# Adding two halves of a softmax's exponents on GpSimd, so that TensorE sums one half, a step later

## The chip, the cores and the metric

One core of one Trainium2 chip runs the whole program. The metric is the device time of one execution in microseconds (us). The core has five engines with queues of their own: TensorE (PE, its weight loads as PEld), VectorE (DVE), ScalarE (ACT), GpSimd (POOL) and SyncE (SP, which here only issues DMAs). They meet at semaphores alone.

## The reference

The kernel computes a gated block over 64 batches of 256 positions by 512 columns, in float32: cross attention with 16 heads of 32 columns on a normalised `x`, then a gated feed-forward part.

```
att = einsum('bthf,byhf->bhty', relu(q), relu(k))      # q = layernorm(x), k = v = ctx
att = softmax(att / sqrt(32), axis=-1)
out = einsum('bhty,byhf->bhtf', att, relu(v))
x = x + tanh(g_xattn) * relu(out @ ffn_w.T + ffn_b)
# second part, on layernorm(x): r = sigmoid(xr @ W_r.T), k = xk @ W_k.T
x = x + tanh(g_ffn) * (r * (square(relu(k)) @ W_v.T))
```

## The kernel before

Each engine runs one function `iteration(i, par)` for i from -3 to 66; the middle ones are a loop over pairs. Inside an iteration the order on each engine is written out by hand, and nothing else sets it: an engine runs its list in order and waits where a semaphore is not yet high enough. Batch i is in attention, batch i-1 in its projection, batch i-2 in the feed-forward part, batch i+1 begins its scores.

TensorE's iteration has 16 steps, each opened by `shifted_scores(i, n)` (L933) for head n = 0 to 15. The other pieces lie between: `scores(i+1, n)` or `scores(i, n)` (L921, whose row maxima VectorE takes), quarters of the dense products `dense(q, part)` (L966), transposes, and for each group c of four heads `values(i, c)` (L947: exponents times values) and `denominators(i, c)` (L959: exponents times ones). The last two write the two halves of one PSUM bank, `pv_bank`. A head's exponents are 128 keys by 2 halves `v` by 256 queries, so both sum over the two key halves by accumulating in PSUM; a group has 8 matmuls for its values and 8 for its denominators, each of which the trace shows as two records.

Who waits for whom around the third group (c = 2) of an iteration:

- ScalarE writes the exponents (L509) into `probs`, half 0 for even groups, half 1 for odd ones.
- VectorE's `norm_o(i, 2)` waits for the third denominators, takes the reciprocal (L737, 1 instruction) and multiplies (L739). Only then may TensorE's `values(i, 3)`, in the next iteration's step 0, overwrite `pv_bank`.
- VectorE's `head_max(i+1, n)` (L718) reduces the scores of L921; `finish(i-2, 0)` is L788 and L791; `k_low` is L707; `q_low` L701; `mix_k` L771, `mix_r` L780; `add_x` begins with L746.
- GpSimd's list ends with `xk_low(i-1, 0)`, `xk_low(i-1, 1)` (both L379) and `o_low(i, 0)` (L361). The second `xk_low` waits for ScalarE's second `xk_high` (L540).
- ScalarE issues `load_v(i+1, 0)`, a DMA, after the third denominators; its `exponent(i, 15)` and `o_high(i, 0)` (L516) stand behind that.
- SP's `write_o(i, 2)` follows `norm_o(i, 2)`.

Of the kernel before, what the change touches and what calls it, by code (L numbers as in the profile page):

```python
# [7 lines left out]
ALU = mybir.AluOpType  # L8
# [8 lines left out]
def flamingo_block(nc, x, ctx_in, ctx_t, g_xattn, g_ffn, w_t, bias, mu, out):  # L17
# [18 lines left out]
    NB, T, D = x.shape  # L36
    HD = D // HEADS
    NU = T // P
    KC = D // P
    GR = P // HD  # L40
    CH = HEADS // GR
    SCALE = float(HD) ** -0.5
    assert NU == 2 and KC == 4 and GR == 4 and CH == 4 and HD == 32
# [4 lines left out]
    with es:  # L48
# [104 lines left out]
        m_copied = sem("m_copied")  # L153
        st_ready = sem("st_ready")
        exp_ready = sem("exp_ready")
        pv_ready = sem("pv_ready")
        rden_ready = sem("rden_ready")
        o_ready = sem("o_ready")
# [174 lines left out]
        def _(pool):  # L333
# [39 lines left out]
            def xk_low(b, half):  # L373
                if on(b):
# [4 lines left out]
                    nc.gpsimd.tensor_tensor(xk_lo[:, part, :], xm[:, part, :], xk_hi[:, part, :].bitcast(F32),  # L379
                                            ALU.subtract).then_inc(xk_lo_ready, 1)  # L380

            def xr_low(b):
                if on(b):
                    pool.wait_ge(xr_ready, b + 1)
                    pool.wait_ge(xr_hi_ready, b + 1)
                    after(pool, r_ready, NU * b)
                    nc.gpsimd.tensor_tensor(xr_lo[:, :, :], xd[:, :, :], xr_hi[:, :, :].bitcast(F32),  # L387
                                            ALU.subtract).then_inc(xr_lo_ready, 1)
# [17 lines left out]
            def iteration(i, par):  # L406
                ka_square(i - 2, 0)
                rstd_1(i + 2)
                ka_square(i - 2, 1)
                o_low(i - 1, 1)  # L410
                xr_low(i - 2)
                rstd_2(i - 1, 0)
                rstd_2(i - 1, 1)
                x_diff(i - 1, 0)
                ka_low(i - 2, 0)
                ka_low(i - 2, 1)
                x_diff(i - 1, 1)
                xk_low(i - 1, 0)
                xk_low(i - 1, 1)
                o_low(i, 0)  # L420

            pipeline(pool, iteration)
# [235 lines left out]
        def _(dve):  # L658
# [135 lines left out]
            def iteration(i, par):  # L794
# [54 lines left out]
                finish(i - 2, 0, par)  # L849

                head_max(i + 1, 5)
                norm_o(i, 2)

                head_max(i + 1, 6)

            dve.wait_ge(setup_act, 2)
            nc.vector.tensor_scalar(tgh[:, :], tg[:, 1:2], 0.5, None, ALU.mult).then_inc(setup_dve, 1)
# [5 lines left out]
        def _(pe):  # L863
# [73 lines left out]
            def values(b, c):  # L937

                if on(b):
                    pe.wait_ge(exp_ready, HEADS * b + GR * c + GR)  # L940
                    pe.wait_ge(v_ready, 2 * b + 1 + c // 3)

                    after(pe, o_ready, CH * b + c)
                    for v in range(NU):
                        for g in range(GR):
                            h = GR * c + g
                            nc.tensor.matmul(pv_bank[HD * g:HD * g + HD, 0:T], v_pos[:, v, HD * h:HD * h + HD],  # L947
                                             probs[:, c % 2, g, v, :], start=(v == 0), stop=(v == NU - 1))

            def denominators(b, c):  # L950


                if on(b):

                    after(pe, o_ready, CH * b + c)
                    sums = [[probs[:, c % 2, g, v, :] for g in range(GR)] for v in range(NU)]
                    for n, per_head in enumerate(sums):
                        for g, moving in enumerate(per_head):
                            mm = nc.tensor.matmul(pv_bank[HD * g:HD * g + HD, T:2 * T], ones_r[:, 0:HD].bitcast(F32),  # L959
                                                  moving, start=(n == 0), stop=(n == len(sums) - 1))  # L960
                    mm.then_inc(pv_ready, 1)
# [65 lines left out]
            def iteration(i, par):  # L1027
# [121 lines left out]
                shifted_scores(i, 14)  # L1149
                dense(7, 0)  # L1150
                scores(i + 1, 5)
                denominators(i, 2)
                dense(7, 1)

                shifted_scores(i, 15)
                dense(7, 2)
                scores(i + 1, 6)
                dense(7, 3)

# [37 lines left out]
```

## Time and profile before

| | |
|---|---|
| median of 3 runs | 2789.77 us (2787.65 to 2789.96) |
| the profiled execution | 2788.89 us, of which 2787.0 us from its first to its last instruction |
| TensorE busy | 2681.2 us, 96% |
| VectorE busy | 2298.6 us, 82% |
| ScalarE busy | 1464.3 us, 53% |
| GpSimd busy | 1079.4 us, 39% |
| DMA | 576.71 MB, mean 207 GB/s |
| mean granted TensorE clock | 0.994 |

The table gives shares over the whole span. Matmuls are pipelined and overlap in the trace, so the end of one lies behind the start of the next; what a piece costs TensorE is read from start to start. The program does the same thing about every 41.4 us, so one iteration, read instruction by instruction, stands for most of the run.

### The profile page before, as it was taken

The numbers are of one execution on the slowest core, as the hardware profiler recorded it, in microseconds if no ns is written. First come the engines' busy times: TensorE is split into PE (matmuls) and PEld (weight loads), VectorE is DVE, ScalarE is ACT, GpSimd is POOL, SyncE is SP. The second block draws the span as 40 slices with busy tenths as digits, with TensorE's granted clock in tenths as the row PEclk, the third lists the DMA queues.
The fourth block names the chain that finished last, engine by engine and source line by source line (L and its number), as shares of the span: only waits on it lengthen the run. The fifth ranks groups of instructions, "written<-read, shape, count | busy, mean of one in ns | idle before, by whom it ended". The sixth has DMA issues, their size and how long they took to land.

```text
span 2787.0 us, 65658 instructions
## 1 busy us (share of the span) xinstructions
PE 2681.2 (96%) x21250; PEld 2056.1 (74%) x21250; DVE 2298.6 (82%) x3981; ACT 1464.3 (53%) x2507; POOL 1079.4 (39%) x902
## 2 busy tenths in 40 slices
PE   1799999999999999999999999999999999999998
PEld 1477777777777777777777777777777777777776
DVE  3778888888888888888888888888888888888864
ACT  2445555555555555555555555555555555555542
POOL 0134334443444433434434434434443444343433
PEclk9899999999999999999999999999999999999999
DMA  7676677677777677677677677777777667767641
GB/s 220 182 214 198 199 225 211 204 236 211 200 231 219 199 231 217 201 228 215 206 221 218 204 222 223 204 217 226 208 208 234 210 202 231 216 201 226 195 121 44
DMA packets 507774, 576.71 MB, mean 207 GB/s; under 512 B 175824, under 2 KB 407248, under 8 KB 507728
## 3 DMA queue, kind: packets, MB, share of 16 engines
q1 hardware_dynamic: 355152, 341.18, 41.7%
q10 hardware_dynamic: 152576, 234.93, 27.9%
q8 instruction: 27, 0.44, 0.1%
q14 instruction: 19, 0.16, 0.0%
HBM read 373.56 MB, written 201.33 MB: 206 GB/s over the span
## 4 chain that ended last, share of the span: by engine, by line
PE 89%; DMA 4%; DVE 2%; SPq 2%; issue 1%; ACT 1%; POOL 1%; ACTq 0%; DVEq 0%; POOLq 0%
PE bank L966 50%; PE bank L933 9%; PE bank L947 9%; PE bank L959 9%; PE bank L921 8%; PE bank L908 3%; PE bank L891 2%; DMA o_mv<-o_dram 2%; PE bank L899 1%; DMA o_dram<-o_val 1%; DMA q_st<-m_t 1%; DVE o_val L737 1%; SPq L291 1%; DVE m_nat L718 0%; ACT xr_hi L546 0%
## 5 line engine op out<-in xcount | busy, mean ns | idle before, releaser
L509 ACT ACTIVATE probs<-bank 128x512 f32<-128x512 f32 x1024 | 610.4, 596 | 898.7 <-PE bank L933 875.1
L718 DVE TENSOR_REDUCE m_nat<-bank 128x2 fp32r<-128x512 f32 x1024 | 687.9, 683 | 119.8 <-PE bank L921 119.2
L737 DVE RECIPROCAL o_val<-bank 128x256 f32<-128x256 f32 x256 | 449.3, 1755 | 108.5 <-PE bank L959 101.7
L921 PE MATMUL bank<-k_st,q_st 96*128 96x256 f32 x2048 | 431.8, 293 | 19.0 <-DVE m_nat L718 12.1
L933 PE MATMUL bank<-q_st,k_st 97*128 97x256 f32 x2048 | 426.4, 290 | 23.6 <-DMA q_st<-m_t 22.7
L933 PEld LDWEIGHTS bank<-q_st,k_st 97*128 97x128 f32 x2048 | 356.4, 191 | 104.2 <-issue 28.4
L921 PEld LDWEIGHTS bank<-k_st,q_st 96*128 96x128 f32 x2048 | 358.3, 192 | 73.0 <-DVE m_nat L718 15.9
L379 POOL TENSOR_TENSOR xk_lo<-xm,xk_hi 128x512 fp32r<-128x512 f32 x128 | 211.4, 1652 | 269.0 <-DVE xm L771 234.7
L394 POOL TENSOR_TENSOR xm<-xm 128x512 f32<-128x512 f32 x128 | 133.8, 1046 | 452.2 <-ACT xm L553 452.1
L966 PE MATMUL bank<-xk_hi,w_hi 128*128 128x256 f32 x1024 | 294.9, 288 | 0.0
L361 POOL TENSOR_TENSOR o_lo<-o_mv,o_hi 128x512 fp32r<-128x512 f32 x128 | 167.6, 1310 | 326.5 <-ACT o_hi L516 320.2
L966 PE MATMUL bank<-xk_hi,w_lo 128*128 128x256 f32 x1024 | 286.6, 280 | 0.0
L966 PE MATMUL bank<-xk_lo,w_hi 128*128 128x256 f32 x1024 | 286.6, 280 | 0.0
L947 PE MATMUL bank<-probs,v_pos 128*32 128x256 f32 x4096 | 275.8, 387 | 1.0 <-DVE o_val L739 1.0
L959 PE MATMUL bank<-probs,ones_r 128*32 128x256 f32 x4096 | 276.3, 387 | 0.0
L353 POOL TENSOR_TENSOR rstd<-ve,mhalf 128x1 f32<-128x1 f32 x128 | 69.2, 540 | 450.5 <-DVE ve L755 450.5
L966 PE MATMUL bank<-w_hi,o_hi 128*128 128x512 f32 x512 | 209.4, 409 | 17.4 <-POOL o_lo L361 17.4
L966 PE MATMUL bank<-w_hi,xr_hi 128*128 128x512 f32 x512 | 209.0, 408 | 4.2 <-POOL xr_lo L387 4.2
L966 PEld LDWEIGHTS bank<-xk_hi,w_hi 128*128 128x128 f32 x1024 | 192.6, 188 | 26.0 <-issue 25.9
L966 PE MATMUL bank<-w_hi,ka_hi 128*128 128x512 f32 x512 | 209.7, 410 | 0.0
L966 PE MATMUL bank<-w_hi,ka_lo 128*128 128x512 f32 x512 | 203.7, 398 | 0.0
L966 PE MATMUL bank<-w_hi,xr_lo 128*128 128x512 f32 x512 | 203.6, 398 | 0.0
(87 smaller groups left out, 5445.1 us busy)
## 6 DMA issues: line engine op xcount, KB each, us to landing
q_st<-q_dram ACTq DMA_DIRECT2D x256, 256.0 KB, 4.9
k_st<-k_dram SPq DMA_DIRECT2D x256, 256.0 KB, 4.6
x_ln<-x_dram SPq DMA_DIRECT2D x256, 128.0 KB
k_raw<-ctx_t_dram SPq DMA_DIRECT2D x256, 128.0 KB, 5.0
q_dram<-q_high ACTq DMA_DIRECT2D x64, 512.0 KB, 3.1
q_dram<-q_raw ACTq DMA_DIRECT2D x64, 512.0 KB, 4.1
k_dram<-k_high SPq DMA_DIRECT2D x64, 512.0 KB, 4.4
k_dram<-k_raw SPq DMA_DIRECT2D x64, 512.0 KB, 5.4
```

Of the source, the lines that this page charges most:

```text
L361: nc.gpsimd.tensor_tensor(by_tile(o_lo, u), o_mv[:, :, :].rearrange("p g (k a) -> p k g a", k=KC), by_tile(o_hi, u).bitcast(F32), ALU.subt ...
L379: nc.gpsimd.tensor_tensor(xk_lo[:, part, :], xm[:, part, :], xk_hi[:, part, :].bitcast(F32), ALU.subtract).then_inc(xk_lo_ready, 1)
L394: nc.gpsimd.tensor_tensor(part, part, part, ALU.mult).then_inc(ka_ready, 1)
L509: nc.scalar.activation(probs[:, n // GR % 2, n % GR, :, :].rearrange("p v t -> p (v t)"), st_bank[n % 2][:, :], ACT.Exp, scale=SCALE).then ...
L718: nc.vector.tensor_reduce(m_nat[:, c % 2, n % GR, :], s_bank[n % 2][:, :].rearrange("p (u y) -> p u y", u=NU), AX_X, ALU.max, negate=True) ...
L737: nc.vector.reciprocal(o_val[:, c % 2, :], pv_bank[:, T:2 * T]).then_inc(rden_ready, 1)
L908: mm = nc.tensor.transpose(tp_bank[:, P * c:P * c + P], xn[:, u, P * c:P * c + P], ident_r[:, :].bitcast(F32))
L921: mm = nc.tensor.matmul(s_bank[n % 2][:, T * u:T * u + T], q_st[0:QK, c, g, P * u:P * u + P], k_st[0:QK, c, g, :], start=True, stop=True)
L933: mm = nc.tensor.matmul(st_bank[n % 2][:, T * v:T * v + T], k_st[0:ST, c, g, P * v:P * v + P], q_st[0:ST, c, g, :], start=True, stop=True)
L947: nc.tensor.matmul(pv_bank[HD * g:HD * g + HD, 0:T], v_pos[:, v, HD * h:HD * h + HD], probs[:, c % 2, g, v, :], start=(v == 0), stop=(v == ...
L959: mm = nc.tensor.matmul(pv_bank[HD * g:HD * g + HD, T:2 * T], ones_r[:, 0:HD].bitcast(F32), moving, start=(n == 0), stop=(n == len(sums) - 1))
L966: mm = nc.tensor.matmul(dst, lhs[a], rhs[c], start=first and n == 0, stop=last and n == 2, skip_group_check=True)
```

## The change

Three edits. GpSimd gets a function `fold(i)`, between the second `xk_low` and `o_low(i, 0)`: after TensorE's third values have read `probs`, it adds the exponents of the second key half to those of the first, in place (128 partitions by 4 heads by 256 queries, 1024 elements in each partition). TensorE's third denominators then sum over the first half alone: 4 matmuls in place of 8; they wait for the fold, and stand in step 15, behind `dense(7, 2)`, in place of step 14. On VectorE `head_max(i+1, 6)` now stands ahead of `norm_o(i, 2)`. Two semaphores are new, `v_used` and `p_folded`.

```diff
@@ -38,6 +38,7 @@
     NU = T // P
     KC = D // P
     GR = P // HD
+    FOLDED = 2
     CH = HEADS // GR
     SCALE = float(HD) ** -0.5
     assert NU == 2 and KC == 4 and GR == 4 and CH == 4 and HD == 32
@@ -153,6 +154,8 @@
         m_copied = sem("m_copied")
         st_ready = sem("st_ready")
         exp_ready = sem("exp_ready")
+        v_used = sem("v_used")
+        p_folded = sem("p_folded")
         pv_ready = sem("pv_ready")
         rden_ready = sem("rden_ready")
         o_ready = sem("o_ready")
@@ -379,6 +382,13 @@
                     nc.gpsimd.tensor_tensor(xk_lo[:, part, :], xm[:, part, :], xk_hi[:, part, :].bitcast(F32),
                                             ALU.subtract).then_inc(xk_lo_ready, 1)
 
+            def fold(b):
+
+                if on(b):
+                    pool.wait_ge(v_used, b + 1)
+                    half = [probs[:, FOLDED % 2, :, v, :] for v in range(NU)]
+                    nc.gpsimd.tensor_tensor(half[0], half[0], half[1], ALU.add).then_inc(p_folded, 1)
+
             def xr_low(b):
                 if on(b):
                     pool.wait_ge(xr_ready, b + 1)
@@ -417,6 +427,7 @@
                 x_diff(i - 1, 1)
                 xk_low(i - 1, 0)
                 xk_low(i - 1, 1)
+                fold(i)
                 o_low(i, 0)
 
             pipeline(pool, iteration)
@@ -849,9 +860,9 @@
                 finish(i - 2, 0, par)
 
                 head_max(i + 1, 5)
+
+                head_max(i + 1, 6)
                 norm_o(i, 2)
-
-                head_max(i + 1, 6)
 
             dve.wait_ge(setup_act, 2)
             nc.vector.tensor_scalar(tgh[:, :], tg[:, 1:2], 0.5, None, ALU.mult).then_inc(setup_dve, 1)
@@ -944,8 +955,10 @@
                     for v in range(NU):
                         for g in range(GR):
                             h = GR * c + g
-                            nc.tensor.matmul(pv_bank[HD * g:HD * g + HD, 0:T], v_pos[:, v, HD * h:HD * h + HD],
-                                             probs[:, c % 2, g, v, :], start=(v == 0), stop=(v == NU - 1))
+                            mm = nc.tensor.matmul(pv_bank[HD * g:HD * g + HD, 0:T], v_pos[:, v, HD * h:HD * h + HD],
+                                                  probs[:, c % 2, g, v, :], start=(v == 0), stop=(v == NU - 1))
+                    if c == FOLDED:
+                        mm.then_inc(v_used, 1)
 
             def denominators(b, c):
 
@@ -953,7 +966,9 @@
                 if on(b):
 
                     after(pe, o_ready, CH * b + c)
-                    sums = [[probs[:, c % 2, g, v, :] for g in range(GR)] for v in range(NU)]
+                    if c == FOLDED:
+                        pe.wait_ge(p_folded, b + 1)
+                    sums = [[probs[:, c % 2, g, v, :] for g in range(GR)] for v in range(1 if c == FOLDED else NU)]
                     for n, per_head in enumerate(sums):
                         for g, moving in enumerate(per_head):
                             mm = nc.tensor.matmul(pv_bank[HD * g:HD * g + HD, T:2 * T], ones_r[:, 0:HD].bitcast(F32),
@@ -1149,11 +1164,11 @@
                 shifted_scores(i, 14)
                 dense(7, 0)
                 scores(i + 1, 5)
-                denominators(i, 2)
                 dense(7, 1)
 
                 shifted_scores(i, 15)
                 dense(7, 2)
+                denominators(i, 2)
                 scores(i + 1, 6)
                 dense(7, 3)
 
```

TensorE's list in the first iteration of the loop, before, from the third `values` (L947) to the next iteration's `values` (a `shifted_scores` is L933, a `scores` L921, a dense quarter three rows of L966):

```order
649 L933 MATMUL bank<-q_st,k_st 128x256 x2
650 L966 MATMUL bank<-w_hi,ka_hi 128x512
651 L966 MATMUL bank<-w_hi,ka_lo 128x512
652 L966 MATMUL bank<-w_lo,ka_hi 128x512
653 L921 MATMUL bank<-k_st,q_st 128x256 x2
654 L959 MATMUL bank<-probs,ones_r 32x256 x8
655 L966 MATMUL bank<-w_hi,ka_hi 128x512
656 L966 MATMUL bank<-w_hi,ka_lo 128x512
657 L966 MATMUL bank<-w_lo,ka_hi 128x512
658 L933 MATMUL bank<-q_st,k_st 128x256 x2
```

and the same stretch after the change, a little further on, where L974 is the denominators, L981 a dense quarter, L944 and L932 the two kinds of scores:

```order
653 L932 MATMUL bank<-k_st,q_st 128x256 x2
654 L981 MATMUL bank<-w_hi,ka_hi 128x512
655 L981 MATMUL bank<-w_hi,ka_lo 128x512
656 L981 MATMUL bank<-w_lo,ka_hi 128x512
657 L944 MATMUL bank<-q_st,k_st 128x256 x2
658 L981 MATMUL bank<-w_hi,ka_hi 128x512
659 L981 MATMUL bank<-w_hi,ka_lo 128x512
660 L981 MATMUL bank<-w_lo,ka_hi 128x512
661 L974 MATMUL bank<-probs,ones_r 32x256 x4
662 L201 REGISTER_ALU
663 L932 MATMUL bank<-k_st,q_st 128x256 x2
```

The third denominators have moved behind two dense quarters and a `shifted_scores`, and are four matmuls. They stand right ahead of `scores(i+1, 6)`.

VectorE's list at the same place, before (L718 is `head_max`, L788 and L791 are `finish(i-2, 0)`, L737 and L739 `norm_o(i, 2)`):

```order
281 L788 SCALAR_TENSOR_TENSOR th<-th,bank 128x512
282 L791 SCALAR_TENSOR_TENSOR x<-th,tgh,x 128x512
283 L713 REGISTER_ALU
284 L718 TENSOR_REDUCE m_nat<-bank 128x2
285 L737 RECIPROCAL o_val<-bank 128x256
286 L739 TENSOR_TENSOR o_val<-bank,o_val 128x256
287 L713 REGISTER_ALU
288 L718 TENSOR_REDUCE m_nat<-bank 128x2
```

and after (L729, L799, L802, L748 and L750 are the same five):

```order
280 L799 SCALAR_TENSOR_TENSOR th<-th,bank 128x512
281 L802 SCALAR_TENSOR_TENSOR x<-th,tgh,x 128x512
282 L724 REGISTER_ALU
283 L729 TENSOR_REDUCE m_nat<-bank 128x2
284 L724 REGISTER_ALU
285 L729 TENSOR_REDUCE m_nat<-bank 128x2
286 L748 RECIPROCAL o_val<-bank 128x256
287 L750 TENSOR_TENSOR o_val<-bank,o_val 128x256
```

The reciprocal and its product now stand behind the maximum of head 6, whose scores TensorE makes after the denominators.

## Rows read from the trace of the kernel before

**Rows 1.** The page: busy us, share and instructions of each engine.
```profile
PE 2681.2 (96%) x21250; PEld 2056.1 (74%) x21250; DVE 2298.6 (82%) x3981; ACT 1464.3 (53%) x2507; POOL 1079.4 (39%) x902
```

**Rows 2.** Busy time by stretch: PE, PEld, DVE, ACT, POOL (instructions), clock, DMA.
```profile
1500.00:1550.00 50.00, 50.00 (x404) 37.80 (x403) 42.34 (x79) 28.42 (x49) 20.05 (x19) 1.00 0.68 203
```

**Rows 3.** Timeline of PE around the third denominators: start, duration, operation.
```profile
1507.25 1.07 PE L959 MATMUL bank<-probs,ones_r 128*32 128x256 f32 x16
...
1517.53 0.40 PE L921 MATMUL bank<-k_st,q_st 96*128 96x256 f32 x2
1517.87 1.07 PE L959 MATMUL bank<-probs,ones_r 128*32 128x256 f32 x16
1518.87 0.50 PE L966 MATMUL bank<-w_hi,ka_hi 128*128 128x512 f32 x1
1519.20 0.40 PE L966 MATMUL bank<-w_hi,ka_lo 128*128 128x512 f32 x1
...
1520.59 0.40 PE L921 MATMUL bank<-k_st,q_st 96*128 96x256 f32 x2
...
1522.82 1.07 PE L947 MATMUL bank<-probs,v_pos 128*32 128x256 f32 x16
```

**Rows 4.** Of the same denominators, the last eight records, then the last four.
```profile
1518.32 0.61 PE L959 MATMUL bank<-probs,ones_r 128*32 128x256 f32 x8
...
1518.54 0.40 PE L959 MATMUL bank<-probs,ones_r 128*32 128x256 f32 x4
```

**Rows 5.** Timeline of POOL at that place.
```profile
1516.75 1.69 POOL L379 TENSOR_TENSOR xk_lo<-xm,xk_hi 128x512 fp32r<-128x512 f32 x1 [0.96 <-issue]
1521.35 1.28 POOL L361 TENSOR_TENSOR o_lo<-o_mv,o_hi 128x512 fp32r<-128x512 f32 x1 [2.91 <-ACT o_hi L516]
```

**Rows 6.** Timeline of DVE at that place, and at the denominators before.
```profile
1508.38 1.76 DVE L737 RECIPROCAL o_val<-bank 128x256 f32<-128x256 f32 x1 [0.37 <-PE bank L959]
...
1516.08 1.20 DVE L707 SCALAR_TENSOR_TENSOR k_raw<-k_raw,k_high 128x1024 fp32r<-128x1024 f32 x1
1518.51 0.75 DVE L791 SCALAR_TENSOR_TENSOR x<-th,tgh,x 128x512 f32<-128x512 f32 x1
1519.18 0.68 DVE L718 TENSOR_REDUCE m_nat<-bank 128x2 fp32r<-128x512 f32 x1
1519.78 1.75 DVE L737 RECIPROCAL o_val<-bank 128x256 f32<-128x256 f32 x1
1521.57 0.42 DVE L739 TENSOR_TENSOR o_val<-bank,o_val 128x256 f32<-128x256 f32 x1
```

**Rows 7.** Groups of POOL by form: count, busy us, mean ns, idle before and releasers.
```profile
L379 POOL TENSOR_TENSOR xk_lo<-xm,xk_hi 128x512 fp32r<-128x512 f32 x128 | 211.4, 1652 | 269.0 <-DVE xm L771 234.7 <-issue 33.7 <-ACT xk_hi L540 0.6
L387 POOL TENSOR_TENSOR xr_lo<-xd,xr_hi 128x1024 fp32r<-128x1024 f32 x64 | 152.4, 2382 | 10.7 <-issue 10.1 <-ACT xr_hi L546 0.2
L394 POOL TENSOR_TENSOR xm<-xm 128x512 f32<-128x512 f32 x128 | 133.8, 1046 | 452.2 <-ACT xm L553 452.1
L370 POOL TENSOR_TENSOR xd<-xt 128x512 f32<-128x512 f32 x128 | 133.2, 1041 | 5.3 <-ACT xt L531 2.2
```

**Rows 8.** Timeline near the end: DVE's L791 beside POOL's two `xk_low`.
```profile
2755.23 2.55 POOL L379 TENSOR_TENSOR xk_lo<-xm,xk_hi 128x512 fp32r<-128x512 f32 x2 [1.71 <-DVE xm L771]
...
2756.51 1.82 DVE L791 SCALAR_TENSOR_TENSOR x<-th,tgh,x 128x512 f32<-128x512 f32 x1
```

**Rows 9.** PE and POOL where PE waits for POOL.
```profile
2575.63 1.26 POOL L361 TENSOR_TENSOR o_lo<-o_mv,o_hi 128x512 fp32r<-128x512 f32 x1 [5.93 <-ACT o_hi L516]
2577.04 0.47 PE L966 MATMUL bank<-w_hi,o_hi 128*128 128x512 f32 x1 [3.06 <-POOL o_lo L361]
```

**Rows 10.** PE at the first group: the scores right behind its denominators.
```profile
1537.46 0.51 PE L933 MATMUL bank<-q_st,k_st 97*128 97x256 f32 x2
```

**Rows 11.** Clock around waits of PE: a stretch with a wait of 2.03, one with 3.06.
```profile
196.00:212.00 16.00, 13.97 (x92) 10.40 (x94) 9.63 (x17) 7.78 (x14) 5.21 (x4) 0.89 0.68 175
2572.00:2584.00 12.00, 8.94 (x63) 6.91 (x63) 6.86 (x13) 7.06 (x13) 4.21 (x3) 1.00 0.62 150
```

## The prediction

> **What bounds the kernel now.** I read the page's busy shares first: TensorE 96%, VectorE 82%, GpSimd 39% [rows 1]. A share over the whole span leaves open whether TensorE ever waits, so next came the busy time by stretch: in the middle of the run TensorE is busy 50.00 of 50.00 us at a granted clock of 1.00 [rows 2]. Its list has no hole there, so what is taken out of it, or made to wait in it, counts in full. Then I read one iteration in order of time, TensorE first and after it the two engines on which the change makes it wait [rows 3, 5, 6]. The reader is to see how little lies between the pieces: GpSimd's second `xk_low` ends at 1516.75 + 1.69 = 1518.44 [rows 5], TensorE begins the third denominators at 1517.87 and the fourth group's `values`, already in the next iteration, at 1522.82 [rows 3], and VectorE ends `norm_o(i, 2)`, for which those values wait, at 1521.57 + 0.42 = 1521.99 [rows 6]. That is 0.83 us to spare.
>
> **What is saved.** The sixteen records of the third denominators take 1.00 us from their start to the next matmul's [rows 3], in packs of four; the last two packs start at 1518.32 and 1518.54 [rows 4], 0.22 apart. Two packs less save 0.44 us an iteration, and 0.56 is left.
>
> **When TensorE would come to the denominators.** Six equal units of dense work and scores stand between 1519.20 and 1520.59 [rows 3], so one takes 0.23. The denominators add 1.00, and beside it 0.11 ahead (1517.53 to 1517.87 is 0.34 for one unit) and 0.10 behind (1518.87 to 1519.20 is 0.33 for one) [rows 3]: 1.21. Taken out of step 14 they let TensorE reach the place ahead of `scores(i+1, 6)` at 1520.59 - 1.21 = 1519.38, and with the 0.11 the moved denominators could start at 1519.48.
>
> **When the fold is done.** It stands behind the second `xk_low` and can't start before 1518.44. That is late for a reason that stays: `xk_low` needs VectorE's `mix_k`, that stands behind `norm_o(i, 1)`, and this waits for TensorE's second denominators in the same iteration (0.37 us idle ahead of L737 at 1508.38, which is 0.06 after 1507.25 + 1.07) [rows 3, 6]. A TensorE that waits in step 15 thus gives GpSimd no lead. The fold's duration is in no row: 1024 elements, float32 written. With `fp32r` written, 512 take 1.28 [rows 5] and 1024 take 2.38 [rows 7], so 0.18 is fixed and 1.10 goes with every 512. With float32 written, 512 take 1.04 (L370, L394) [rows 7]; less 0.18 that is 0.86, and twice 0.86 with 0.18 is 1.90. I take 1.90, as the fold writes float32 like these two. It can't be under the 1.04 of half the elements, and 2.38 is the nearest whole operation of that size; these are its ends. So it ends at 1520.34, and a TensorE that waits for GpSimd starts 0.15 later (2575.63 + 1.26 = 2576.89, then 2577.04) [rows 9]: at 1520.49, a wait of 1.01 us.
>
> For this size the Trainium skill has a price of its own: GPSIMD Engine Reference, section "Performance versus the Vector engine", gives an add of 2048 float32 elements 4497 ns some 2.6 cycles an element, and calls that the floor for two inputs; half of 4497 is an estimate of 2.25 us. The 1.04 of 512 elements with float32 written [rows 7] lies under a quarter of it (1.12). By the page each iteration would lose 0.35 more, and the run would end at 2915.
>
> **What VectorE does meanwhile.** L791 of `finish` starts at 1518.51 [rows 6], with the fold. It reads two SBUF tensors, and such an instruction and GpSimd's do not run side by side: beside `xk_low`, which ends at 2755.23 + 2.55 = 2757.78, L791 took from 2756.51 to 2758.33, 1.82 in place of the 0.75 that it takes alone [rows 6], and ended 0.55 after it [rows 8]; the other way round, `xk_low` began at 1516.75 inside `k_low` (L707, 1516.08 to 1517.28) and ended 1.16 after that one's end, for an operation that alone takes 1.28 [rows 5, 6]. Whoever starts second waits. The fold is 0.07 us ahead, so L791 ends at 1520.34 + 0.55 = 1520.89 and `head_max(i+1, 5)` about 0.6 later, at 1521.5. I cost this at nothing, since the next maximum has to wait for TensorE anyhow, as follows.
>
> **The second wait.** Behind the denominators (1520.49) `scores(i+1, 6)` start 0.56 later, at 1521.05, and last 0.51, as scores behind denominators do [rows 10]: 1521.56. `head_max(i+1, 6)`, now ahead of `norm_o(i, 2)`, starts 0.06 after, at 1521.62, and gives way 0.60 later (1519.18 to 1519.78) [rows 6]; `norm_o` takes 1519.78 to 1521.99, 2.21 [rows 6], and ends at 1524.43. `values(i, 3)` start at 1524.49. Unhindered TensorE would be there 0.56 + 0.10 + 2.23 (1520.59 to 1522.82) after the denominators [rows 3], at 1523.38; it waits 1.11.
>
> **The sum.** `values(i, 3)` move from 1522.82 to 1524.49, +1.67 us, which is 1.01 + 1.11 - 0.44. From there the iteration is as before: the next denominators and `norm_o(i, 3)` follow at the same distance. What else moves has room: ScalarE's `load_v` waits for the later denominators, and `exponent(i, 15)`, `o_high` and GpSimd's `o_low` stand behind it. Before, `o_low` started 2.41 after the denominators' end (1518.94 to 1521.35) [rows 3, 5]; at that distance it starts at 1523.5 and ends at 1524.8, ahead of `norm_o(i, 3)`, which needs it and can't come before `values(i, 3)` and the denominators behind it, 1.07 and 1.07 long [rows 3]. On SP `write_o(i, 2)` is later by 2.4, and behind it stands a `move_m` that depends on a still later maximum. Of 64 iterations I count 62, as the first and the last have not all their neighbours: 62 x 1.67 = 104 us. The profiled execution took 2788.89, so 2892; the median of the runs is 0.88 above it, so 2893. With the fold at 1.04 an iteration loses 0.81 (2840), with 2.38 it loses 2.15 (2923).
>
> **Rivals.**
> - VectorE gets the memory first. The fold's lead is 0.07 us, and its first read may come later than its start. Then it stands until L791 ends at 1519.26 and, like `xk_low`, needs 0.12 less than its 1.90 from there: 1521.04, 0.70 later than above; 2.37 an iteration, 147 in all, 2937. For it speaks the narrow lead, against it that the fold has by then nothing else to wait for. 14%.
> - The fold is hidden, and only VectorE's new order costs. It would have to end by 1519.33, 0.89 us after it can start, less than 512 elements take [rows 7]. TensorE then starts the denominators at 1519.48, `values(i, 3)` come at 1523.48, +0.66: 41 us, 2831. 7%.
> - Faster: TensorE's waits let the other engines get ahead, neither wait is left, and the saved 0.44 shows: 62 x 0.44 = 27, 2762. For it speaks that GpSimd is 39% and VectorE 82% busy [rows 1]; it decides once `xk_low` ends a good 1.0 earlier in TensorE's terms and `norm_o` 1.1 earlier. Against it stands the wait of VectorE for the second denominators [rows 6], which ties them to TensorE every time. 5%.
> - The clock falls as well. After a wait of TensorE of 2.03 us the granted clock was 0.89 over 16.00 us, some 1.8 us lost, and after one of 3.06 it stayed 1.00 [rows 11]. The two waits here are about half as long, 3 us apart. If every second iteration paid it, 55 us more: 2948. 6%.
>
> **Chances and range.** The forecast has 66%, the four rivals 14, 7, 5 and 6, and 2% is for waits and saving that balance. A difference under 0.2%, some 5.6 us, can't be told from no change here. Slower by more than that: forecast, first, second and fourth rival, 93%; within it 2%; faster 5%. The likeliest case alone runs from 2871 to 2923 (a fold of 1.55 to 2.38); with the first rival's 2937 and some room at the lower end for a shorter fold the range is 2850 to 2945, and the hidden fold, the clock and the faster case are left outside.
>
> **What would show it.** In the profile after: TensorE idle ahead of the third denominators, released by GpSimd's fold, some 1.0 us each time; idle again ahead of the values, released by L739's successor, some 1.1; a fold of about 1.9 us; L791's successor at a mean of about 1.6 in place of 0.75, as one of its two per iteration takes some 2.4; the granted clock still near 1. A fold over 2.5 us with an unchanged L791 is the first rival. No wait ahead of the denominators makes the prediction wrong, and no wait ahead of the values makes it wrong by two thirds.

## The result, and the profile after

The changed kernel takes 2902.05 us (median of 4 runs, 2900.70 to 2902.94) against 2789.39 us of the kernel before (4 runs, 2787.65 to 2789.96): a ratio of 1.0405, 95% interval 1.0389 to 1.0420. The forecast was 2893 within 2850 to 2945, so the direction and nearly the size are as foretold. The profiled execution took 2901.61 us, its span 2899.5.

The page's busy line and the chain that ended last, of the changed kernel, and below the same chain before (the busy line before is [rows 1]):

```profile
PE 2656.5 (92%) x20738; PEld 2032.9 (70%) x20738; DVE 2449.3 (84%) x3981; ACT 1462.0 (50%) x2507; POOL 1231.6 (42%) x966
...
PE 62%; DVE 14%; issue 11%; POOL 5%; DMA 2%; ACT 2%; ACTq 2%; SPq 1%; DVEq 0%; POOLq 0%
```

```profile
PE 89%; DMA 4%; DVE 2%; SPq 2%; issue 1%; ACT 1%; POOL 1%; ACTq 0%; DVEq 0%; POOLq 0%
```

TensorE does 24.7 us less, in 512 instructions less, and the run is 112.5 us longer: its share falls from 96% to 92%. GpSimd has 152.2 us more, the 64 additions, and VectorE 150.7 more without one instruction more: its old ones got longer, L802 alone (L791 before) by 123. The same stretch as in [rows 2] shows the granted clock at 1.00 as before, and TensorE no longer full:

```profile
1500.00:1550.00 50.00, 47.67 (x395) 36.85 (x389) 43.74 (x73) 25.39 (x44) 18.95 (x16) 1.00 0.72 209
```

The missing 2.33 us are two waits. TensorE's waits by releaser over the whole run (in total, times, longest), then two of those before:

```profile
PE bank L974 <- POOL probs L390: 83.3, 62, 3.1
PE bank L958 <- DVE o_val L750: 69.0, 64, 2.1
...
PE bank L981 <- POOL o_lo L364: 5.1, 3, 2.4
```

```profile
PE bank L966 <- POOL o_lo L361: 17.4, 9, 3.1
...
PE bank L947 <- DVE o_val L739: 1.0, 1, 1.0
```

The first is the wait for the addition ahead of the third denominators, the second the wait for the reciprocal's product ahead of `values(i, 3)`. Before, the first didn't exist and the second came once in the whole run. One iteration of TensorE (L974 denominators, L932 `scores`, L958 `values`; compare [rows 3]):

```profile
1499.85 1.07 PE L958 MATMUL bank<-probs,v_pos 128*32 128x256 f32 x16 [1.11 <-DVE o_val L750]
...
1525.72 1.07 PE L974 MATMUL bank<-probs,ones_r 128*32 128x256 f32 x16
...
1539.36 0.64 PE L974 MATMUL bank<-probs,ones_r 128*32 128x256 f32 x8 [1.31 <-POOL probs L390]
1539.93 0.51 PE L932 MATMUL bank<-k_st,q_st 96*128 96x256 f32 x2
...
1543.35 1.07 PE L958 MATMUL bank<-probs,v_pos 128*32 128x256 f32 x16 [1.02 <-DVE o_val L750]
```

From the second denominators' start to the values it is now 1543.35 - 1525.72 = 17.63 us; before it was 1522.82 - 1507.25 = 15.57 [rows 3]. GpSimd beside it (L382 `xk_low`, L390 the addition; compare [rows 5]):

```profile
1535.24 1.66 POOL L382 TENSOR_TENSOR xk_lo<-xm,xk_hi 128x512 fp32r<-128x512 f32 x1 [0.96 <-issue]
1536.86 2.35 POOL L390 TENSOR_TENSOR probs<-probs 128x1024 f32<-128x1024 f32 x1
1541.90 1.26 POOL L364 TENSOR_TENSOR o_lo<-o_mv,o_hi 128x512 fp32r<-128x512 f32 x1 [2.69 <-ACT o_hi L527]
```

The addition starts the moment the second `xk_low` ends and takes 2.35 us. TensorE starts 0.15 us behind its end. VectorE (L802 `finish`, L729 `head_max`, L748 and L750 `norm_o`; compare [rows 6]):

```profile
1536.97 2.80 DVE L802 SCALAR_TENSOR_TENSOR x<-th,tgh,x 128x512 f32<-128x512 f32 x1
1539.69 1.48 DVE L729 TENSOR_REDUCE m_nat<-bank 128x2 fp32r<-128x512 f32 x2
1541.08 1.75 DVE L748 RECIPROCAL o_val<-bank 128x256 f32<-128x256 f32 x1
1542.87 0.43 DVE L750 TENSOR_TENSOR o_val<-bank,o_val 128x256 f32<-128x256 f32 x1
```

L802 starts 0.11 behind the addition, ends 0.56 behind it (1539.77 against 1539.21) and takes 2.80 where it takes 0.75 alone. The two maxima run back to back, and the reciprocal starts without a pause behind them. L802's delay costs nothing here, though: the scores of head 6 end at 1539.93 + 0.51 = 1540.44, and with the 0.06 and 0.60 us of [rows 3, 6] from there to the maximum and on to the reciprocal, the latter would start at about 1541.10 in any case. By groups over the whole run, the last line before the change:

```profile
L390 POOL TENSOR_TENSOR probs<-probs 128x1024 f32<-128x1024 f32 x64 | 151.2, 2362 | 31.2 <-PE bank L958 31.2
...
L802 DVE SCALAR_TENSOR_TENSOR x<-th,tgh,x 128x512 f32<-128x512 f32 x128 | 220.7, 1725 | 4.5
```

```profile
L791 DVE SCALAR_TENSOR_TENSOR x<-th,tgh,x 128x512 f32<-128x512 f32 x128 | 97.7, 763 | 4.5
```

From the fourth group's `values` to the next iteration's, the changed kernel takes 1543.35 - 1499.85 = 43.50 us; before, from the 1522.82 of [rows 3], it was 1564.23 - 1522.82 = 41.41:

```profile
1564.23 1.07 PE L947 MATMUL bank<-probs,v_pos 128*32 128x256 f32 x16
```

Neighbouring iterations differ a little, in turns. Of the full iterations (7 to 59 of the 64, 53 of them) nearly every one took 41.41 or 41.44 before and takes 43.48 to 43.60 now, so 41.42 and 43.54 stand for them, 2.12 apart. One of those before took 42.11, so all 53 together grew by 111.5 us, 2.10 each, out of 112.5. The other iterations and both ends add up to 1 us: there the kernel before already lost time to `o_low`. Of its 17.4 us of that wait, 0.4 stand in the middle of the run (at 1414 us, in the iteration of 42.11) and the rest at the ends; the changed kernel has 5.1.

### The profile page after: what moved, and what is told of

The parts are those of the page before. It is cut to its first block, busy times and chain, and to the rows that moved or that the text cites. A ratio compares the mean times of both kernels' runs of the same rounds, so it can differ in the third digit from the quotient of the medians.

```text
span 2899.5 us, 64790 instructions
## 1 busy us (share of the span) xinstructions
PE 2656.5 (92%) x20738; PEld 2032.9 (70%) x20738; DVE 2449.3 (84%) x3981; ACT 1462.0 (50%) x2507; POOL 1231.6 (42%) x966
## 4 chain that ended last, share of the span: by engine, by line
PE 62%; DVE 14%; issue 11%; POOL 5%; DMA 2%; ACT 2%; ACTq 2%; SPq 1%; DVEq 0%; POOLq 0%
PE bank L981 32%; PE bank L974 8%; DVE o_val L748 8%; PE bank L958 7%; PE bank L944 6%; PE bank L932 6%; POOL probs L390 5%; DVE m_nat L729 3%; PE bank L902 2%; ACTq L475 2%; PE bank L919 1%; DVE o_val L750 1%; DVE xm L782 1%; ACT th L588 1%; PE bank L910 1%
## 5 line engine op out<-in xcount | busy, mean ns | idle before, releaser
L729 DVE TENSOR_REDUCE m_nat<-bank 128x2 fp32r<-128x512 f32 x1024 | 693.5, 683 | 121.5 <-PE bank L932 110.5
L748 DVE RECIPROCAL o_val<-bank 128x256 f32<-128x256 f32 x256 | 449.3, 1755 | 86.3 <-PE bank L974 85.9
L932 PE MATMUL bank<-k_st,q_st 96*128 96x256 f32 x2048 | 438.4, 296 | 15.5 <-DVE m_nat L729 10.5
L944 PE MATMUL bank<-q_st,k_st 97*128 97x256 f32 x2048 | 425.8, 289 | 24.3 <-DMA q_st<-m_t 24.2
L944 PEld LDWEIGHTS bank<-q_st,k_st 97*128 97x128 f32 x2048 | 357.0, 191 | 103.8 <-issue 27.5
L932 PEld LDWEIGHTS bank<-k_st,q_st 96*128 96x128 f32 x2048 | 353.9, 192 | 89.5 <-issue 31.3
L958 PE MATMUL bank<-probs,v_pos 128*32 128x256 f32 x4096 | 275.8, 387 | 69.0 <-DVE o_val L750 69.0
L382 POOL TENSOR_TENSOR xk_lo<-xm,xk_hi 128x512 fp32r<-128x512 f32 x128 | 213.0, 1664 | 268.6 <-DVE xm L782 235.1
L974 PE MATMUL bank<-probs,ones_r 128*32 128x256 f32 x3584 | 248.7, 388 | 83.3 <-POOL probs L390 83.3
L981 PE MATMUL bank<-xk_hi,w_hi 128*128 128x256 f32 x1024 | 295.6, 289 | 0.0
L981 PE MATMUL bank<-xk_hi,w_lo 128*128 128x256 f32 x1024 | 287.0, 280 | 0.0
L981 PE MATMUL bank<-xk_lo,w_hi 128*128 128x256 f32 x1024 | 287.0, 280 | 0.0
L958 PEld LDWEIGHTS bank<-probs,v_pos 128*32 128x32 f32 x4096 | 110.4, 109 | 192.3 <-issue 68.3
L802 DVE SCALAR_TENSOR_TENSOR x<-th,tgh,x 128x512 f32<-128x512 f32 x128 | 220.7, 1725 | 4.5
L974 PEld LDWEIGHTS bank<-probs,ones_r 128*32 128x32 f32 x3584 | 92.9, 109 | 175.2 <-issue 133.4
L981 PE MATMUL bank<-w_hi,xr_hi 128*128 128x512 f32 x512 | 209.3, 409 | 4.2 <-POOL xr_lo L397 4.2
L981 PE MATMUL bank<-w_hi,o_hi 128*128 128x512 f32 x512 | 208.0, 406 | 5.1 <-POOL o_lo L364 5.1
L981 PEld LDWEIGHTS bank<-xk_hi,w_hi 128*128 128x128 f32 x1024 | 193.0, 189 | 26.0 <-issue 25.9
```

The lines of the kernel that those rows point to most:

```text
L729: nc.vector.tensor_reduce(m_nat[:, c % 2, n % GR, :], s_bank[n % 2][:, :].rearrange("p (u y) -> p u y", u=NU), AX_X, ALU.max, negate=True) ...
L748: nc.vector.reciprocal(o_val[:, c % 2, :], pv_bank[:, T:2 * T]).then_inc(rden_ready, 1)
L802: nc.vector.scalar_tensor_tensor(out=x1[:, par, u, :], in0=th[:, u, :], scalar=tgh[:, 0:1], in1=x1[:, par, u, :], op0=ALU.mult, op1=ALU.ad ...
L932: mm = nc.tensor.matmul(s_bank[n % 2][:, T * u:T * u + T], q_st[0:QK, c, g, P * u:P * u + P], k_st[0:QK, c, g, :], start=True, stop=True)
L944: mm = nc.tensor.matmul(st_bank[n % 2][:, T * v:T * v + T], k_st[0:ST, c, g, P * v:P * v + P], q_st[0:ST, c, g, :], start=True, stop=True)
L958: mm = nc.tensor.matmul(pv_bank[HD * g:HD * g + HD, 0:T], v_pos[:, v, HD * h:HD * h + HD], probs[:, c % 2, g, v, :], start=(v == 0), stop= ...
```

## The experiments

Eleven kernels were timed, and one run measured GpSimd's addition by itself. "Iteration" below is the full iteration as just told; 41.42 us is that of the kernel before. Each ratio is to the kernel before, timed beside the run in question.

**The second wait alone.** The changed kernel without the addition, with all eight matmuls in the denominators:

```diff
                 xk_low(i - 1, 1)
-                fold(i)
                 o_low(i, 0)
...
-                    if c == FOLDED:
-                        pe.wait_ge(p_folded, b + 1)
-                    sums = ... for v in range(1 if c == FOLDED else NU)]
+                    sums = ... for v in range(NU)]
```

> The kernel after without the fold: the third denominators sum both halves (8 matmuls) in step 15, and VectorE's head_max(i+1, 6) stands ahead of norm_o(i, 2). Theory of two waits: no wait ahead of the denominators, but the values still wait for norm_o, some 1.15 us later in every undisturbed iteration than before; with 53 such iterations 61 us, 2850. Rival, the fold alone costs and the new place and order are free: 2789.

Measured: 2858.55 us, ratio 1.0252 (1.0219 to 1.0285); iteration 42.5 to 42.6 in nearly all. The wait for `norm_o` is there 64 times, with no addition to cause it:

```profile
PE bank L957 <- DVE o_val L749: 69.0, 64, 2.1
```

So the later place and VectorE's new order cost some 1.15 us an iteration by themselves. The prediction's order-only rival (2831) counted 0.66 for them, with the saved half still in it: 0.66 + 0.44 = 1.10.

**The first wait without the second.** The changed kernel with `norm_o(i, 2)` ahead of `head_max(i+1, 6)` again:

```diff
-                head_max(i + 1, 6)
                 norm_o(i, 2)
 
+                head_max(i + 1, 6)
```

> The kernel after with VectorE's old order: norm_o(i, 2) ahead of head_max(i+1, 6). Theory of two waits: the wait for the fold stays at 1.3 us, norm_o begins behind the held-up L791 and head_max(i+1, 5), and the wait ahead of the values falls from 1.1 to 0.3; an iteration 1.33 longer than before in place of 2.12, some 2860 to 2868. Rival, the order of the two does not matter because both wait for the same denominators: 2902.

Measured: 2867.59 us, ratio 1.0287 (1.0253 to 1.0322); iteration 42.95. TensorE waits for the addition as in the changed kernel, and hardly for VectorE (L802 is still held up beside the addition, so this run has the shared memory access in it as well):

```profile
PE bank L975 <- POOL probs L390: 83.3, 62, 3.1
...
PE bank L959 <- DVE o_val L750: 8.2, 33, 0.8
```

**The saving alone.** The kernel before, whose third denominators read one half, with no addition, so that their sums leave out the second half of the keys:

```diff
-                    sums = [[probs[:, c % 2, g, v, :] for g in range(GR)] for v in range(NU)]
+                    sums = [[probs[:, c % 2, g, v, :] for g in range(GR)] for v in range(1 if c == 2 else NU)]
```

> The kernel before with the third denominators over the first half alone, in their old place, with no fold (it leaves out the second half of the keys in one group's denominators). Theory: four matmuls are worth 0.43 us of an undisturbed iteration and nothing takes it back, 23 to 27 us in all, 2763 to 2766. Rival, TensorE gives it back in another wait: 2785 to 2790.

A miss. Four matmuls less an iteration, and nothing added, made it slower: 2859.17 us, ratio 1.0249 (1.0200 to 1.0298), with runs from 2848 to 2871. Iterations lie anywhere from 41.00 to 46.8. TensorE waits for `o_low`, which stands behind the trip of `norm_o`'s output through DRAM (`write_o`, `read_o`, `o_high`):

```profile
PE bank L966 <- POOL o_lo L361: 83.6, 51, 3.4
```

```profile
ACT o_hi L516 <- DMA o_mv<-o_dram: 290.2, 124, 6.0
```

where ScalarE's wait before was:

```profile
ACT o_hi L516 <- DMA o_mv<-o_dram: 91.9, 68, 5.7
```

The chain that ended last, 89% TensorE before, is now:

```profile
PE 54%; DMA 18%; DVE 14%; issue 6%; SPq 4%; ACT 3%; DVEq 1%; POOL 0%; ACTq 0%; POOLq 0%
```

So a second bound, the way of `o` through DRAM, lies within half a microsecond of TensorE's. Such a bound explains why nothing was gained; why the iterations got longer than the old 41.42 and so uneven, it doesn't explain. Four more runs, below, look for what sets the bound.

**The shared memory access alone.** The kernel before, with the same addition at the same place, written to a buffer that nobody reads (`q_nat`, free there); TensorE's list is the old one:

```diff
                 xk_low(i - 1, 1)
+                fold(i)
                 o_low(i, 0)
...
+                    nc.gpsimd.tensor_tensor(spare, half[0], half[1], ALU.add).then_inc(p_folded, 1)
```

> The kernel before with an add of the fold's size at the fold's place in GpSimd's list, written into another tile, so that nobody needs it. Theory that GpSimd's add and L791 can't run side by side: L791 ends 2.05 us later, head_max(i+1, 5) and norm_o(i, 2) follow, and the values wait for norm_o, 1.33 us an iteration, 70 in all, 2860. Rival, an add that nobody reads costs nothing: 2789.

Measured: 2867.99 us, ratio 1.0280 (1.0248 to 1.0312); iteration 1.55 longer. Nothing that TensorE or VectorE does next needs this sum (`q_nat` and `probs` are only guarded against being written again too early, and no wait of VectorE or ScalarE for the addition shows); it delays VectorE all the same, and TensorE waits for VectorE. GpSimd, then VectorE (L807 is `finish`, L753 the reciprocal, L755 its product), then TensorE's wait:

```profile
1518.92 2.37 POOL L391 TENSOR_TENSOR q_nat<-probs 128x1024 f32<-128x1024 f32 x1
```

```profile
1519.03 2.82 DVE L807 SCALAR_TENSOR_TENSOR x<-th,tgh,x 128x512 f32<-128x512 f32 x1
1522.38 1.74 DVE L753 RECIPROCAL o_val<-bank 128x256 f32<-128x256 f32 x1
```

```profile
PE bank L963 <- DVE o_val L755: 57.9, 62, 1.4
```

So these two engines do not meet at semaphores alone: an instruction of one lengthens that of the other with no wait for a semaphore between them. The new order and place cost 2.5% by themselves, the shared access 2.8%, and the wait for the sum together with the shared access 2.9%; they don't add up to the changed kernel's 4.05%. There the order's 1.15 and the wait's 1.34 us, less the saved 0.42 (measured below), give 2.07 of the 2.12 an iteration, which leaves nothing for L802, whose delay lies in the time in which VectorE would wait for TensorE's scores anyhow.

**How long an addition takes on GpSimd.** Additions of 512 and 1024 elements ahead of the main loop, with the operands and the output varied:

> The kernel before with 22 adds on GpSimd in its setup, where it is idle, each kind twice: 512 elements a+a, a plus a shifted by one element, a+e (another tile), a+a and a+e written as fp32r, a+e in place; 1024 elements a+a, a+e in place, the fold's own pattern, and the fold's pattern with both inputs the first half. The prediction's reason (float32 written is quicker than fp32r): 1.04, 1.04, 1.04, 1.28, 1.28, 1.04 us for 512, and 1.90 for 1024 except where the fold's pattern costs. Rival, two inputs from the same place are quicker than two from different ones: 1.04, 1.04, 1.28, 1.04, 1.28, 1.28, then 1.9, 2.35, 2.35, 1.9.

Measured, by output and inputs (count, then ns of the shortest, the median and the longest, the first and the last start, the shapes):

```profile
L364 POOL TENSOR_TENSOR o_val<-q_nat x4: 1037/1038/1039, 9.5 to 12.8; 128x512 f32<-128x512 f32 x4
L364 POOL TENSOR_TENSOR q_nat<-q_nat,q_raw x4: 1261/1800/2337, 21.5 to 30.6; 128x512 f32<-128x512 f32 x2, 128x1024 f32<-128x1024 f32 x2
...
L364 POOL TENSOR_TENSOR o_val<-q_nat,q_raw x2: 1260/1261/1262, 14.0 to 15.3; 128x512 f32<-128x512 f32 x2
L364 POOL TENSOR_TENSOR xk_hi<-q_nat x2: 1037/1037/1037, 16.6 to 17.8; 128x512 fp32r<-128x512 f32 x2
L364 POOL TENSOR_TENSOR xk_hi<-q_nat,q_raw x2: 1259/1260/1260, 18.9 to 20.2; 128x512 fp32r<-128x512 f32 x2
L364 POOL TENSOR_TENSOR q_raw<-q_nat x2: 1891/1891/1891, 24.2 to 26.2; 128x1024 f32<-128x1024 f32 x2
```

The type written makes no difference: 1.04 with float32 and with `fp32r` where one tile is read, 1.26 with either where two are. What costs is a second place to read: 1.26 against 1.04 us for 512 elements, 2.34 against 1.89 for 1024. Two of the four additions in the first row read the tile and the same tile one element further on, and these are as cheap as the other two. The two key halves lie further apart and cost as two tiles do:

```profile
33.00 2.34 POOL L364 TENSOR_TENSOR probs<-probs 128x1024 f32<-128x1024 f32 x1
...
39.80 1.89 POOL L364 TENSOR_TENSOR probs<-probs 128x1024 f32<-128x1024 f32 x1
```

The first adds the two halves, the second one half to itself. The forecast's 1.90 is the price of the second kind.

**The shorter addition in the changed kernel.**

```diff
-                    nc.gpsimd.tensor_tensor(half[0], half[0], half[1], ALU.add).then_inc(p_folded, 1)
+                    nc.gpsimd.tensor_tensor(half[0], half[0], half[0], ALU.add).then_inc(p_folded, 1)
```

> The changed kernel with one operand of the add exchanged: GpSimd adds the first key half of the exponents to itself, so the second half is left out of the sums and the sums are wrong. The addition stays where it is, with the same size, the same output and the same readers; by the probe it then takes 1.89 us in place of 2.34. Theory, the add stands on the path and its length passes one to one into each full iteration: 0.45 us x 53 = 24 us less than the changed kernel, about 2878 (2870 to 2886), the add ends at 13.05 behind the second denominators' start instead of 13.50. Rival, another engine sets the pace by then (VectorE's copies behind the add, or the o path's DMA): within 8 us of 2902.

The second half is left out of these sums. Measured: 2874.76 us, ratio to before 1.0305 (1.0275 to 1.0336), 27 under the changed kernel; iteration 43.09 (median), 0.45 less than 43.54. GpSimd, VectorE:

```profile
1528.09 1.88 POOL L390 TENSOR_TENSOR probs<-probs 128x1024 f32<-128x1024 f32 x1
```

```profile
1528.20 2.33 DVE L802 SCALAR_TENSOR_TENSOR x<-th,tgh,x 128x512 f32<-128x512 f32 x1
```

L802 shrinks by the same 0.47. The addition is on the path and its length passes through one to one.

**What the second bound is: moving the keys' write.** SP writes 1 MB of keys to DRAM (`write_k`) between `read_o(i, 0)` and `write_o(i, 2)`. In two kernels it was issued behind the next iteration's `read_o(i-1, 1)`, once with the half denominators, once in the kernel before:

```diff
                 read_o(i - 1, 1)
+                write_k(i + 1, 1 - par)
+                move_m(i, 2)
                 keys_written(i + 1)
...
                 read_o(i, 0)
-                write_k(i + 2, par)
                 write_o(i, 2)
```

> The kernel with half the third denominators in their old place (wrong sums in one group, no fold) and in addition SP issuing write_k, 1 MB, behind read_o(i-1, 1) of the next iteration, in place of ahead of write_o(i, 2). Theory that the shorter TensorE list lost to o_mv because the DMA engines are full when write_o(i-1, 3) is issued: with 1 MB out of the way TensorE no longer waits for o_lo, and the saving shows: 2745 to 2765. Rival, the wait for o_lo comes from the shorter list itself (norm_o, ScalarE), whatever the DMAs: 2850 to 2860 as without.

> The kernel before with write_k issued behind read_o(i-1, 1) of the next iteration, nothing else. Theory of the full DMA engines: the steady iteration has no wait for o_lo and stays at 41.42 us, the first and last ones lose their 12 to 17 us of waits: 2772 to 2780. Rival, write_k is no part of it: 2785 to 2795; or it now delays k_st and x_1, and TensorE waits for those: over 2800.

Measured: 2891.53 us with the half, ratio 1.0351 (1.0330 to 1.0371), and 2894.09 in the kernel before, ratio 1.0368 (1.0339 to 1.0397). Both missed, and the edit made a wait of its own: `move_m`, 4 KB, now goes behind the 1 MB. With the half denominators:

```profile
PE bank L933 <- DMA q_st<-m_t: 108.5, 62, 9.8
...
PE bank L966 <- POOL o_lo L361: 7.7, 5, 2.5
```

The time says nothing for or against the theory that the DMAs ahead hold the `o` trip up. The second row fits it, with the wait for `o_low` at 7.7 us in place of 83.6, but doesn't prove it: a TensorE that is late itself leaves that trip more time.

**Moving the output's store.** `store(i-3)`, 512 KB, stands ahead of `write_o(i-1, 3)`, 128 KB, on SP's queue. SP in the kernel before and with the half denominators (L298 `store`, L282 `write_o`, L291 `read_o`, which waits for the write to land):

```profile
1524.75 0.40 SPq L298 DMA_DIRECT2D out_dram<-x  x1
1527.36 0.34 SPq L282 DMA_DIRECT2D o_dram<-o_val  x1
1529.64 1.80 SPq L291 DMA_DIRECT2D o_mv<-o_dram  x4
```

```profile
1517.76 0.41 SPq L298 DMA_DIRECT2D out_dram<-x  x1
1520.12 0.34 SPq L282 DMA_DIRECT2D o_dram<-o_val  x1
1522.79 2.04 SPq L291 DMA_DIRECT2D o_mv<-o_dram  x4
```

From `write_o` to `read_o` it is 2.28 us before and 2.67 with the half in these two iterations; over fifty in the middle of each run the medians are 2.14 and 3.11. Two kernels issue the store behind `write_o`, with the half denominators and without:

```diff
-                store(i - 3, 1 - par)
                 move_m(i, 1)
                 write_o(i - 1, 3)
+                store(i - 3, 1 - par)
                 read_o(i - 1, 1)
```

> The kernel with half the third denominators in their old place (wrong sums in one group, no fold), and SP issuing store(i-3), 512 KB, behind write_o(i-1, 3) in place of ahead of move_m(i, 1). Theory that the shorter list lost its gain because write_o(i-1, 3), 128 KB, lands behind the store on SP's queue: the read of o starts some 1 us earlier, TensorE's wait for o_lo falls from 83.6 us to under 20, 2755 to 2790. Rival, the DMA engines are full whatever the order: 2845 to 2870 as without. Second rival, the later store holds up ScalarE's load_x1: over 2870.

> The kernel before with store(i-3) behind write_o(i-1, 3), nothing else. Theory: the steady iteration stays at 41.42 us, the waits of the first and last iterations for o_lo (17.4 us) mostly go, 2772 to 2782. Rival, the order on the queue is nothing: 2784 to 2793.

Measured: 2750.92 us with the half, ratio 0.9872 (0.9843 to 0.9900), iteration 41.01; and 2774.73 without, ratio 0.9951 (0.9936 to 0.9967), iteration 41.43. SP with the half, then TensorE's wait for `o_low`:

```profile
1504.88 0.33 SPq L282 DMA_DIRECT2D o_dram<-o_val  x1
1505.42 0.40 SPq L298 DMA_DIRECT2D out_dram<-x  x1
1506.83 1.88 SPq L291 DMA_DIRECT2D o_mv<-o_dram  x4
```

```profile
PE bank L966 <- POOL o_lo L361: 8.6, 5, 2.4
```

Here the read follows 1.95 us behind the write, 1.78 in the median of fifty. The waits fall from 51 to 5, the run comes out a little below the 2755 to 2790 expected, and the half shows its whole worth: 41.43 - 41.01 = 0.42 an iteration, 24 us a run, against the prediction's 0.44. This settles the second bound: what SP has put in front of `write_o`. That the 128 KB wait behind the 512 KB can be read from the two traces with the store ahead: in fifty middle iterations of the kernel before, the write landed 0.28 to 0.45 us behind the store, whenever the store had landed, and with the half 0.29 to 0.86 behind; with the store behind it (and all denominators) it landed 1.69 to 1.79 us after its issue. The Trainium skill's page DMA: Bandwidth & Descriptors, section "Queues, rings and completion order", says that a DMA engine takes a queue's descriptors in the order of its ring; these landings agree. With the half the store itself took 4.96 us to land, 4.43 before (medians); why, and with it why that run got slower than before, stays open. In the kernel before, the store's place costs some 13 us, nearly all at the two ends of the run, where the `o` trip is late.

**A version that uses the addition.** The addition between the two `xk_low` (where GpSimd idles), `k_low` ahead of `copy_m(i+1, 0)`, `norm_o` ahead of `head_max(i+1, 6)`; first with the denominators behind `shifted_scores(i, 15)`, then behind `dense(7, 2)` and with the store moved (the diff shows the addition's place alone):

```diff
                 xk_low(i - 1, 0)
-                xk_low(i - 1, 1)
                 fold(i)
+                xk_low(i - 1, 1)
                 o_low(i, 0)
```

> The kernel after with the fold between the two xk_low, VectorE's k_low ahead of copy_m(i+1, 0), norm_o(i, 2) ahead of head_max(i+1, 6), and the third denominators behind shifted_scores 15. Theory: the fold starts at 9.1 us after the second denominators in place of 11.1 and ends at 11.4, TensorE comes at 11.5; neither wait is left and the list is 0.43 us shorter than before. Then TensorE should wait for o_lo as with half the denominators alone: 2830 to 2860. Rival, the shorter list alone: 2762.

> The fold between the two xk_low, k_low ahead of copy_m(i+1, 0), norm_o(i, 2) ahead of head_max(i+1, 6), the third denominators behind dense(7, 2) as in the kernel after, and store(i-3) behind write_o(i-1, 3). Theory: the fold ends at 11.9 after the second denominators, TensorE comes at 12.3 and waits for nothing there; norm_o lets the values start 0.2 us earlier than before; with o on time 2760 to 2780. Rival, the wait for o_lo stays (99.6 us with the store ahead): 2860 to 2910.

Measured: 2916.43 us, ratio 1.0456 (1.0435 to 1.0477), for the first, and 2780.06, ratio 0.9970 (0.9956 to 0.9983), for the second. The first missed: the addition runs into `k_low` and takes 3.38 us, TensorE waits 28.4 us for it, and 99.6 us for `o_low`:

```profile
1502.84 3.38 POOL L390 TENSOR_TENSOR probs<-probs 128x1024 f32<-128x1024 f32 x1
```

The second waits for the addition only twice in the run, 2.5 us in all. Its iteration is 41.37, only 0.06 under the kernel before, with a new wait of 9.7 us for VectorE's maxima, and its interval overlaps that of the moved store by itself: without its waits the addition gives no gain that these runs can tell from none. The lowest time of a version that computes the whole reference is that of the kernel before with the store moved, 2774.73 us.

## Why the prediction was right

- **Two new waits, where it put them: right.** Ahead of the third denominators TensorE was foretold to wait 1.01 us, released by the addition, and ahead of the values 1.11, released by `norm_o`. Measured are 83.3 us over 62 times, 1.34 each, and 69.0 over 64, 1.08 each. The two runs with one wait each show that either stands without the other.
- **When the addition starts: right.** Foretold 1518.44 - 1507.25 = 11.19 us behind the second denominators' start; measured 1536.86 - 1525.72 = 11.14. It was first at the memory in 61 of the 62 iterations in which the two meet, so L802 waits and the first rival (2937) did not come true. Foretold was that L802 ends 0.55 behind the addition; it ends 0.56 behind. That this delay costs nothing in the changed kernel was right too (1541.10 against 1541.08 above), though where TensorE doesn't wait for the addition the same delay costs 1.55 an iteration.
- **How long it takes: the step that failed.** The 1.90 came out of the thought that the `fp32r` written makes `xk_lo` and `xr_lo` dearer. The probe refutes it: the type costs nothing. The two cheap operations of [rows 7] read one place: L394 multiplies `xm` by itself, and L370 subtracts `xt` from `xt` one element further on. The rejected 2.38, upper end of the term, was the nearest operation in size and in inputs, and nearly exact (2.36 on average). The Trainium skill's page GPSIMD Engine Reference, section "Performance versus the Vector engine", gave the prediction an estimate of 2.25, nearer than 1.90; the trace decides for 2.36. The run with the same half twice shows the price of the mistake: 0.45 us an iteration, 27 us a run.
- **The size of the whole iteration: right, once the duration is put in.** For 2.38 the prediction had 2.15 us more an iteration; 2.12 came. It took 62 iterations at the full price, and only 53 pay it; in most of the others the `o` trip had set the pace before. 62 x 1.67 = 104 and 53 x 2.10 = 111: the two faults stand against each other, and the forecast owes it to luck that it missed by no more than 9 us. A sum with the right duration and the wrong count would have said 2923 or so.
- **The saving: right as a term, wrong as a promise.** 0.44 us per iteration is in the sum, and 0.42 was measured where nothing else stands in the way. The "faster" rival let the same 0.44 show as 2762 once the waits were gone; the run with nothing but the half says 2859. The sentence "its list has no hole there, so what is taken out of it [...] counts in full" holds in one direction only: what is added counts in full, what is taken out counts as far as the next bound. That bound was in the rows on which the prediction drew for other ends: [rows 9] and the two waits of [rows 11] are waits of TensorE, and that of [rows 9] is one for `o_low`. A sign nearer by stood in the trace: a wait for `o_low` in the middle of the run.
- **The order-only rival (2831): its price right, its case refuted.** It needed an addition that nobody waits for, and TensorE waited for it 62 times. Its own term, without the saving, gives 1.10, and the run of the move alone shows 1.15 an iteration.
- **The clock: as forecast.** The mean granted clock is 0.996 (0.994 before), and 1.00 in the stretch shown, with two waits in every iteration.

## What to carry to other kernels

Where an engine is busy 50 of 50 us, work added to it costs its whole length, but work taken off it gains only as far as the next bound: before work is taken off, look for the engine or queue that comes next, in the rare waits, here nearly all at the run's ends, where the same chain is a little slower. Price an operation by a row with as many distinct places to read, not by one with the same output. And work moved onto an engine that shares its memory access with another can cost although nobody waits for its result (here 1.55 us an iteration), or nothing, where the other would have waited anyhow: the rows of both engines tell which.

## What the runs showed of the hardware

- A GpSimd addition of 512 float32 elements in each partition took 1.04 us with both operands from one place, or one element apart, and 1.26 from two tiles; 1024 took 1.89 from one place, 2.34 from two tiles or from the two halves of one. The output's type (float32 or fp32r) made no difference.
- GpSimd and VectorE, each with an instruction that reads SBUF twice, did not run side by side: VectorE's 0.75 us became 2.80 beside an addition of 2.35 and 2.33 beside one of 1.88 (of one place read twice), and ended 0.55 us behind it in both; the addition's 2.35 became 3.38 when `k_low` had begun before it.
- Four matmuls less an iteration made a run of this program 2.5% slower and irregular, its iterations 41.0 to 46.8 us long; with the order of two DMAs on one queue exchanged it was 1.3% faster. With the 512 KB ahead of them on that queue, 128 KB landed 0.28 to 0.45 us behind the 512 KB, time after time; ahead of them they took 1.69 to 1.79.
